# Decoder of two layers: in the context attention of layer one, each head's transposed probabilities are written into the PSUM bank that held its scores

## The reference

```python
xn = _layer_norm(x, g1, b1)
cn = _layer_norm(context, g2, b2)
q = xn @ Wq
k, v = jnp.split(cn @ Wkv, 2, axis=-1)
# split into 8 heads of 64
sim = jnp.einsum('bhid,bhjd->bhij', q, k) * scale
attn = jax.nn.softmax(sim, axis=-1)
out = jnp.einsum('bhij,bhjd->bhid', attn, v)
return out.reshape(b, n, INNER) @ Wout + bout
```

## Time and profile before

| | us |
|---|---|
| median of 3 runs | 1822.67 (1822.57 to 1828.09) |
| profiled execution, own time | 1826.97 |
| its span, first to last instruction | 1825.3 |
| context attention of layer one, about | 1071 to 1480 |
| one sequence in its middle | 24.25 |
| mean granted clock of PE | 0.952 |

### The profile page before, as it was taken

One profiled execution on the slowest core, in us unless ns is written; L12 is line 12 of the kernel. 1 busy time (PEld: TensorE's weight loads), 2 busy tenths in 40 slices (PEclk: granted clock), 3 DMA queues, 4 the chain that ended last, 5 costly groups with the idle time before them and its releaser, 6 DMA issues. The chain is left out here.

```text
span 1825.3 us, 36539 instructions
## 1 busy us (share of the span) xinstructions
PE 1645.2 (90%) x12703; PEld 1360.2 (75%) x12703; DVE 1118.3 (61%) x2667; ACT 885.8 (49%) x2544; POOL 558.4 (31%) x864
## 2 busy tenths in 40 slices
PE   5997599999998887599999869999999989999998
PEld 3665467777776576488888757777777779999987
DVE  4776467777777433377776645667666554444464
ACT  2333255555555133155555524444444456666644
POOL 2112222444443234322221121222332256444410
PEclk8999699999999799799999979999999989999999
DMA  8000323444450353100000020000000032213001
GB/s 252 0 0 1 117 78 119 129 127 127 127 169 12 130 167 118 44 14 14 17 12 1 1 87 19 17 18 18 18 18 1 1 127 82 70 70 137 2 1 41
DMA packets 87277, 114.29 MB, mean 63 GB/s; under 512 B 4788, under 2 KB 76680, under 8 KB 86888
## 3 DMA queue, kind: packets, MB, share of 16 engines
q1 hardware_dynamic: 82008, 99.56, 16.9%
q0 software_dynamic: 5136, 12.98, 2.1%
HBM read 64.68 MB, written 47.84 MB: 62 GB/s over the span
## 5 line engine op out<-in xcount | busy, mean ns | idle before, releaser
L1029 ACT ACTIVATE c_probs<-ps,c_negmax 112x375 f32<-112x375 f32 x256 | 143.7, 581 | 2.1 <-DVE c_negmax L1135 2.1
L1240 PEld LDWEIGHTS ps<-const,c_probs 112*125 112x125 f32 x768 | 97.8, 193 | 47.3 <-DVE c_pT L1157 27.5
L1135 DVE TENSOR_REDUCE c_negmax<-ps 112x2 f32<-112x750 f32 x128 | 114.2, 934 | 25.7 <-PE ps L1271 25.7
L1240 PE MATMUL ps<-const,c_probs 112*125 112x112 f32 x768 | 116.1, 289 | 3.6 <-ACT c_probs L1029 2.4
L1988 PE MATMUL ps<-xnT,s_qkv 128*128 128x224 f32 x512 | 112.7, 370 | 4.6 <-ACT e_gate_up L1777 4.1
L1793 ACT ACTIVATE s_probs<-ps,s_negmax 112x112 f32<-112x112 f32 x256 | 86.7, 364 | 36.4 <-DVE s_negmax L1851 36.4
L1988 PEld LDWEIGHTS ps<-xnT,s_qkv 128*128 128x128 f32 x512 | 96.3, 196 | 10.8 <-ACT e_gate_up L1777 5.7
L1330 PE MATMUL ps<-parts 128*125 128x256 f32 (+1 forms) x480 | 91.0, 327 | 5.5 <-DVE X L1086 2.4
L2903 DVE TENSOR_TENSOR e_hid_low<-xnT,e_hid_high 128x528 fp32r<-128x528 f32 x56 | 41.1, 733 | 83.5 <-ACT e_hid_high L2803 83.5
L1017 ACT COPY c_pT<-ps 125x672 f32<-125x672 f32 x64 | 46.1, 720 | 82.1 <-PE ps L1240 82.1
L1330 PEld LDWEIGHTS ps<-parts 128*125 128x125 f32 (+1 forms) x480 | 71.7, 196 | 13.0 <-DVE c_kT L1081 4.4
(11 more groups left out here) (473 smaller groups left out, 5088.1 us busy)
## 6 DMA issues: line engine op xcount, KB each, us to landing
expert_rows<-d_zero SPq DMA_DIRECT2D x16, 2240.0 KB
c_ctx_in<-in_ctx SPq DMA_DIRECT2D x32, 375.0 KB
e_x_in<-expert_rows SPq DMA_DIRECT2D x43, 128.0 KB, 2.1
expert_rows<-e_y POOLq DMA_DIRECT2D x43, 128.0 KB, 2.1
e_w_gate_even<-in_L_ffn_w_gate SPq DMA_DIRECT2D x4, 1024.0 KB, 5.1
e_w_fc_even<-in_L_ffn_w_c_fc SPq DMA_DIRECT2D x4, 1024.0 KB, 7.3
e_w_proj_even<-in_L_ffn_w_c_proj SPq DMA_DIRECT2D x4, 1024.0 KB, 9.8
c_kv<-in_L_ffn_w_gate SPq DMA_DIRECT2D x4, 1024.0 KB, 5.0
```

Source lines behind the costliest of these rows:

```text
L1029: last = nc.scalar.activation(probs[:, g % 2, r, :], ps[:T, r, 0:S], ACT.Exp, bias=negmax[:, par, h:h + 1], accum_out=sums[:, par, h:h + 1])
L1135: nc.vector.tensor_reduce(negmax[:, par, h:h + 3:2], ps[:T, 2 * piece:2 * piece + 2, 0:S], AX.X, ALU.max, negate=True).then_inc(max_done, 1)
L1240: last = nc.tensor.transpose(ps[:KC, bank + r % 2, k * T:(k + 1) * T], probs[:, g % 2, r, k * KC:(k + 1) * KC], ident[:T, :T])
```

## The change

The transposes of head x go to bank x, in which the scores of that head lay, instead of bank 4, and the copies read from there. The wait for `pT_ready` of the head before is taken out of `transposes`; the wait for `exp_done` of the own head stays. The two waits of `values` and `scores` are as before. No instruction is added, removed or moved on any engine, and their sizes stay; only the addresses and one wait change. Bank 4 is left unused in this stage.

```diff
-    BANK_PT, BANK_O, BANK_SIDE = 4, 5, 6
+    BANK_O, BANK_SIDE = 5, 6
...
             def copy_probs(i, g, x):
                 if within(i):
                     act.wait_ge(pT_mm, 4 * (2 * i + g) + x + 1)
-                    nc.scalar.copy(pT[:, x, :], ps[:KC, BANK_PT, 0:SC]).then_inc(pT_ready, 1)
+                    nc.scalar.copy(pT[:, x, :], ps[:KC, x, 0:SC]).then_inc(pT_ready, 1)
...
             def copy_probs(i, g, x):
                 if within(i):
                     dve.wait_ge(pT_mm, 4 * (2 * i + g) + x + 1)
-                    nc.vector.tensor_copy(pT[:, x, :], ps[:KC, BANK_PT, 0:SC]).then_inc(pT_ready, 1)
+                    nc.vector.tensor_copy(pT[:, x, :], ps[:KC, x, 0:SC]).then_inc(pT_ready, 1)
...
                 n = 4 * (2 * i + g) + x
                 pe.wait_ge(exp_done, n + 1)
-                if not (first(i, g) and x == 0):
-                    pe.wait_ge(pT_ready, n)
                 for k in range(NK):
-                    last = nc.tensor.transpose(ps[:KC, BANK_PT, k * T:(k + 1) * T], probs[:, x, k * KC:(k + 1) * KC], ident[:T, :T])
+                    last = nc.tensor.transpose(ps[:KC, x, k * T:(k + 1) * T], probs[:, x, k * KC:(k + 1) * KC], ident[:T, :T])
                 last.then_inc(pT_mm, 1)
```

## The result

The changed kernel takes 1815.01 us (median of 7 runs, 1810.79 to 1819.26), the kernel before 1822.67 in the same comparison (7 runs). The ratio is 0.9947, 95% interval 0.9933 to 0.9961: 9.7 us faster (7 to 12). A second comparison of the same two gave 0.9954 (0.9934 to 0.9974). The profiled execution took 1810.79 us with a span of 1809.1.

What follows compares the result with a forecast made beforehand. PE was taken to set the pace, busy 48.40 of 50 us. Gains of 4.9 + 0.30 + 0.81 + 1.47 + 1.62 = 9.1 us, plus 1.6 for the clock, made 10.7: 1812.0 us from 1822.67, range 1806 to 1819.

Steps and rivals of the forecast that it cites:

- The middle: Group 1, head 3, i = 0 to 13: 0.65 us wait becomes 0.30 at `value2`; 14 x 0.35 = 4.9 us.
- i = 14: Sequence 14: 0.30 us gained in group 0, where `key0` waits behind `take_best`, and 0.81 us in group 1.
- i = 15, group 0: Last sequence: `values` bound by DVE's copy behind `take_best`, starting at 1460.60 instead of 1462.07; 1.47 us gained.
- The clock: PE's two low-clock stretches in i = 15: 1.6 us taken as gained, bounds 0 and 5.0.
- the first low stretch: i = 15, 3.4 us from 1462.10 at 0.53 of full clock: becomes fast, 1.6 us gained.
- The second stretch: i = 15, 6.8 us from 1472.50 at 0.50 of full clock: left as it is, worth up to 3.4 us.
- i = 15, group 1 and the end: Last sequence, group 1: `inverse_logits` bound by the inverse sums, at 1470.44 against 1472.06; 1.62 us gained.
- The sum: Whole kernel: 9.1 us at unchanged clock plus 1.6 for the clock, 10.7 us, giving 1812.0 us.
- All is given back: Rival: `value2` does not wait, 13.3 us gained, 18.3 with both clock stretches; 1804 to 1809; chance 0.09.
- Keeps its size: Rival: the stall moves undiminished in the 14 sequences; only the end gains, 4.2 us, about 1818.5; chance 0.13.
- the rival: DVE and POOL obstruct each other at `c_cn`, each of three pieces taking 1.65 us: +14, about 1836; chance 0.04.

Runs made afterwards that it cites:

- context_first: Changed kernel with the `context1` transposes issued ahead of those of head 2 instead of behind them; ratio 0.9912 to the kernel before, 16.0 us faster.
- the second pair of profiles: The kernel before and the changed kernel, each run again without edit; stage 387.43 and 377.17 us, ratios to before 0.9998 and 0.9954.
- dve_tail: Changed kernel; in the last sequence DVE copies head 2 of group 0 ahead of `first_statistics` and `take_best`; ratio 0.9929 to the kernel before.
- bank_only: Transposes go to the bank of their scores, but the wait for the former head's copy stays; ratio 1.0007 to the kernel before.
- after: The changed kernel in its first comparison and profile; ratio 0.9947 to the kernel before, 1815.01 us against 1822.67.
- after_again: The changed kernel run once more without edit, with its own profile; ratio 0.9954 to the kernel before.
- the experiment on it: Changed kernel; in the last sequence the third piece of expert weights is rounded by ACT and split by POOL about 7 us earlier; ratio 0.9937 to before.

## Why the prediction was right

**The middle: right, undersized.** The stall did not vanish but moved to `value2`, behind ACT's second read of `context1`. I had 0.30 us for the new wait and 0.35 us gained per sequence; it was 0.25 us and 0.42, over the 14 sequences 5.5 us and not 4.9. The mis-sized step is the release: I put 0.14 us between the end of a copy and PE, as behind DVE's copy in the earlier trace rows. ACT's read ends at 1367.97 and `value2` starts at 1368.02, 0.05 us. The forecast had `value2` 1.89 us behind `context1` (1378.35 - 1376.46), it was 1.80, and these 0.09 us are the difference of the two releases. The kernel before shows both releases behind the same engine, ACT, at i = 15: 0.14 us to transposes (1459.61 to 1459.75), and 0.05 to `values` (1462.02 to 1462.07).

```profile
1459.17 0.44 ACT L2337 COPY c_pT<-ps 125x336 f32<-125x336 f32 x1 [0.77 <-PE ps L2577]
1459.75 0.55 PE L2577 MATMUL ps<-const,c_probs 112*125 112x112 f32 x3 [0.62 <-ACT c_pT L2337]
...
1461.58 0.44 ACT L2337 COPY c_pT<-ps 125x336 f32<-125x336 f32 x1 [1.97 <-PE ps L2577]
```

So the release goes with the group that waits, not with the engine that releases it. context_first shows the cause of the new wait by taking it away: the wait is gone and the sequence loses a further 0.31 us.

**i = 14: right.** 23.73 became 22.50, 1.23 us, against 0.30 + 0.81 = 1.11; in the second pair of profiles group 0 gives 0.40 and group 1 0.82. The whole wait in group 0 did not come back, as said: `key1` waits 0.74 us for DVE.

**i = 15, group 0: right in cause.** `values` hang on DVE's copy behind `take_best`, which dve_tail confirms. From the scores to `values` it was 8.27 us (1462.07 - 1453.80) and is 6.58 (1447.61 - 1441.03): 1.69 gained, against 1.47. The copy starts at 1447.06, 0.09 us before `take_best` ends, which I had set end to end, and the release was 0.06 and not 0.14. My sum also had a slip of 0.04: 1459.92 + 0.50 + 0.14 is 1460.56, not 1460.60.

**The clock: the choice held, its cause only in part.** I took the first low stretch as gone and the second as staying. The first was gone in all eight profiles without the waits of i = 15. It was worth 1.63 us, as forecast: `values` took 1.37 and not 2.37, the scores behind them 1.52 and not 2.15. That the waits bring it is not settled, since bank_only had them and no low clock. The second stretch came and went with the same kernel: 15 b at 0.96 in after, at 0.77 in after_again. In the whole study 15 b was above 0.90 only in after and context_first, so leaving it out of the sum was the better choice, and its absence in after is luck. The Trainium skill (TensorE: Matmul & The Clock Gate, "What's actually happening") has activity release the throttle; 11 of the 12 profiles agree for the first stretch, bank_only does not, and for the second they decide nothing.

**i = 15, group 1 and the end: the size right, a bound overlooked.** `inverse_logits` waits for the inverse sums, as said, 0.21 us. From the scores to it were 7.69 us (1472.06 - 1464.37) and are 5.45 (1454.36 - 1448.91), 2.24 less. Of this 0.63 is the clock of the scores, and 1.61 is left, against 1.62. Behind that I had nothing; it gave 0.87 us in after. There PE stood idle 1.35 us before the slots' products. The profile names no releaser, but POOL's `d_oneh` ends at 1457.80, 0.10 us before them. POOL's last split is 1.1 us behind ACT's last copy. That the stage's end follows whichever of the two is last is read from all twelve profiles; the experiment on it moved POOL in a profile in which ACT was last.

**The sum.** 10.7 us were forecast for the stage; the two pairs of profiles give 12.5 and 10.3. In the whole time it is 9.7 (7 to 12) by the ratio, and 7.7 by the medians, so 1815.01 and not 1812.0. That these 3 us are spread of unchanged code is likely but not shown. For it: the experts' stage took 342.2 to 342.5 us in four profiles, 344.6 to 344.9 in six, and 341.2 and 346.5 in the other two, with kernels that keep waits and kernels that don't among both the short and the long.

**The rivals.** "All is given back" fell with the 0.25 us at `value2`. "Keeps its size" fell with 23.83. DVE and POOL did not get more in each other's way at `c_cn`: its three instructions took 1.28 to 1.65 us together in the 13 sequences that have them, where the rival needed 1.65 for each, and `c_oT` waits for PE. The same mechanism did show where I put POOL's work beside another DVE copy. The Trainium skill (SBUF — State Buffer, "Who interferes with whom") lists a copy among the operations that can take the port pair shared with GpSimd; the 0.43 us that became 1.60 agree with it. The blocking did outlast one of POOL's instructions, though, which the prediction had ruled out: 1.60 - 0.43 = 1.17 us more, and a split takes 0.72.

## What to carry to other kernels

When a wait is taken out, follow the engine that it held to the next semaphore, and compare the chain that feeds that one with the time gained; here ACT's two reads kept 0.25 of 0.65 us, and moving the aside that feeds them ahead of three transposes took this wait away too. The few iterations at the end, where the covering work is missing, can be worth as much as all of the middle: 6.2 and 5.4 us here. Where unchanged stages scatter by more than the effect, measure it between two fixed points around the changed stage.

## What the runs showed that was not expected

- From the end of a copy to the PE group that waits for it pass 0.14 to 0.16 us where the group is the transposes of the probabilities or `inverse_logits`, and 0.04 to 0.06 where it is the side work's keys and values, or `values`. This holds over the twelve profiles, behind ACT and behind DVE; why is open.
- The time up to the first scores, in code that no kernel here changes, ran from 1088.1 to 1094.4 us over twelve profiles. That is more than the middle's whole gain of 5.5.
- One DVE copy, 112x512, took 0.43 us in the last sequence of ten profiles, and 0.84 and 1.60 in the two in which POOL's splits were put beside it.
